# Six places for the down weights, rotations behind the scan pieces, and transposes around the last evaluation in a decoder layer

## The reference

```python
x = x + attn(layernorm(x))                 # 16 heads of 32, 2 key/value heads, rotary, causal softmax, then wo
x = x + mamba(ctx, z=layernorm(x))         # below
x = x + ffn(layernorm(x))                  # below

# mamba: ctx (4, 512, 256) -> inner width 512, 16 states
u  = silu(causal_conv4(ctx @ in_proj.T) + conv_b)
dt, B, C = split(u @ x_proj.T);  dt = softplus(dt @ dt_proj.T + b)
for each position: state = state * exp(dt * A) + (dt * u) * B;  y = sum over 16 states of state * C
y = (y + D * u) * silu(z)

# ffn: hidden 1408 = 11 tiles of 128, 8 experts of rank 16, top 2 per token
g, v = x @ Wg.T, x @ Wu.T
out = (silu(g) * v) @ Wd.T
out += sum over experts e of w_e * 2 * (silu(g + 2*x@Ag_e.T@Bg_e.T) * (v + 2*x@Au_e.T@Bu_e.T)) @ Ad_e.T @ Bd_e.T
```

## Time and profile before

| what | value |
|---|---|
| median of the runs | 1496.59 us |
| the profiled execution, its own time | 1496.58 us |
| its span | 1494.8 us |
| TensorE busy (matmul) | 1345.9 us, 90% |
| VectorE busy | 1028.1 us, 69% |
| ScalarE busy | 695.4 us, 47% |
| down matmuls (L934), 352 records | 164.1 us busy, 17.0 us idle before |
| granted TensorE clock, mean | 0.917 of full |

### The profile page before, as it was taken

One profiled execution on the slowest core, in us unless ns is written; L12 is line 12 of the kernel. 1 busy time (PEld: TensorE's weight loads), 2 busy tenths in 40 slices (PEclk: granted clock), 3 DMA queues, 4 the chain that ended last, 5 costly groups with the idle time before them and its releaser, 6 DMA issues.

```text
span 1494.8 us, 16001 instructions
## 1 busy us (share of the span) xinstructions
PE 1345.9 (90%) x5768; PEld 661.1 (44%) x5768; DVE 1028.1 (69%) x1219; ACT 695.4 (47%) x1477; POOL 89.2 (6%) x116
## 2 busy tenths in 40 slices
PE   5757668999999799899999799899999899799999
PEld 2324444444444365444444365444444355444443
DVE  5699996689979645789897844779897944521110
ACT  5345653465542285375552277365562187121110
POOL 0000001000000000000000000100000000100000
PEclk8955669999999799999999889999999999799999
DMA  6286661157765700137765610117775530012102
GB/s 232 46 197 145 136 146 29 53 138 189 189 148 126 176 2 1 43 106 181 180 162 141 164 45 2 39 53 189 190 166 144 144 83 2 0 33 63 59 25 85
DMA packets 53277, 158.80 MB, mean 106 GB/s; under 512 B 5072, under 2 KB 10704, under 8 KB 44752
## 3 DMA queue, kind: packets, MB, share of 16 engines
q0 software_dynamic: 9216, 67.11, 22.6%
q1 hardware_dynamic: 25664, 54.23, 11.1%
q10 hardware_dynamic: 18320, 36.45, 8.1%
HBM read 86.20 MB, written 4.46 MB: 61 GB/s over the span
## 4 chain that ended last, share of the span: by engine, by line
PE 68%; DVE 20%; ACT 6%; DMA 3%; issue 3%; ACTq 0%; POOL 0%; DVEq 0%
PE ps_a L854 21%; PE ps_a L866 10%; DVE state L1048 7%; PE ps_a L934 6%; PE ps_b L874 5%; PE ps_a L780 4%; PE ps_w L833 4%; PE ps_w L742 4%; PE ps_b L794 3%; DMA y_sb<-state 3%; DVE state L1053 3%; DVE state L1043 3%; ACT r L583 2%; DVE neg_max L1083 2%; PE ps_w L900 2%
## 5 line engine op out<-in xcount | busy, mean ns | idle before, releaser
L854 PE MATMUL ps_a<-xt,w_sb 128*128 128x512 f32 x704 | 319.2, 607 | 0.0
L1048 DVE TENSOR_TENSOR_SCAN state<-decay,state 128x2048 f32<-128x2048 f32 x64 | 282.7, 4418 | 2.1 <-DVE state L1043 0.5
L854 PEld LDWEIGHTS ps_a<-xt,w_sb 128*128 128x128 f32 x704 | 137.2, 196 | 173.2 <-issue 172.8
L635 ACT ACTIVATE r<-ps_a 128x512 f32<-128x512 f32 x132 | 78.8, 597 | 257.5 <-PE ps_a L866 137.5
L583 ACT ACTIVATE r<-ps_a,neg_max 128x128 f32<-128x128 f32 (+3 forms) x256 | 134.6, 542 | 131.8 <-DVE neg_max L1083 126.0
L1219 DVE TENSOR_TENSOR r<-r,ps_a 128x512 f32<-128x512 f32 x132 | 90.2, 685 | 149.9 <-ACT r L635 149.9
L934 PE MATMUL ps_a<-wd_sb,r 128*128 128x512 f32 x352 | 164.1, 617 | 17.0 <-DMA wd_sb<-in_w_down 16.8
L541 ACT ACTIVATE decay<-dt_sb,decay_rate 128x511 f32<-128x511 f32 x256 | 163.4, 711 | 30.1 <-DVE state L1048 29.7
L866 PE MATMUL ps_a<-r,wb_sb 128*128 128x512 f32 x352 | 166.6, 596 | 2.2 <-DVE r L1219 2.2
L780 PE MATMUL ps_a<-r 32*128 32x512 f32 (+3 forms) x512 | 125.7, 572 | 44.1 <-ACT r L583 40.0
L1043 DVE TENSOR_TENSOR state<-du_sb,bc_sb 128x2048 f32<-128x2048 f32 x64 | 146.2, 2284 | 7.8 <-DMA y_sb<-state 5.7
(11 more groups left out here) (117 smaller groups left out, 1385.3 us busy)
## 6 DMA issues: line engine op xcount, KB each, us to landing
y_sb<-state POOLq DMA_DIRECT2D x64, 1024.0 KB, 9.3
bc_sb<-bc_rows ACTq DMA_DIRECT2D x64, 512.0 KB, 6.1
w_sb<-in_w_tiles SPq DMA_DIRECT2D x44, 512.0 KB, 8.7
wd_sb<-in_w_down SPq DMA_DIRECT2D x44, 256.0 KB, 3.2
wb_sb<-in_w_adapt SPq DMA_DIRECT2D x44, 128.0 KB, 2.1
xa<-in_x SPq DMA_DIRECT2D x4, 1024.0 KB, 5.2
out_x<-xb SPq DMA_DIRECT2D x16, 256.0 KB, 8.0
xn_att<-in_ctx_t SPq DMA_DIRECT2D x4, 512.0 KB, 7.9
```

Of the source, the lines that this page charges most:

```text
L854: mm = nc.tensor.matmul(ps_a[:, 2 * (f % 2) + half, :], w_sb[:, slot, at + k * P:at + (k + 1) * P], xt[:, k, :], start=(k == 0), stop=Fals ...
L1048: nc.vector.tensor_tensor_scan(flat, decay[:, n % 2, :, :].rearrange("p j l -> p (j l)"), flat, 0.0, ALU.mult, ALU.add).then_inc(scan_chai ...
```

## The change

There are four edits. (1) The down weights get six places instead of two: the two of `wd_sb` and the four halves of `w_sb`, which is no longer read after the wide matmuls of tiles 9 and 10. Tiles 2 and 3 are loaded when tile 9's wide products are done, tiles 4 and 5 when tile 10's are, the later ones when the matmuls of the tile six before are done. (2) In the first stage and in the middle batches VectorE's `rotate` of a slot stands behind the slot's scan pieces. (3) Of the four transposes of the next input, TensorE does two ahead of the last evaluation's adapter matmuls and two behind them, and ScalarE moves two ahead of the last gate. (4) Where the scan of a state runs in slot `DOWN`, its decay is made in that slot: of all plans this moves one item, the decay of state 10, from the slot of evaluation 31 to slot 33 in `PLAN_NEXT`.

```diff
+WD_RING = 6
@@ plan
-        slots[at["du", 0] if n == 0 else between(at["du", 0] if n == 1 else at["run", n - 2], at["run", n])]["decay"].append(n)
+        first = at["du", 0] if n < 2 else at["run", n - 2]
+        slots[first if n == 0 else DOWN if at["run", n] == DOWN else between(first, at["run", n])]["decay"].append(n)
@@
+        wd_ring = [wd_sb[:, 0, :], wd_sb[:, 1, :], w_sb[:, 1, 0:D], w_sb[:, 1, D:2 * D],
+                   w_sb[:, 0, 0:D], w_sb[:, 0, D:2 * D]]
@@ sync: load_wd
-                if f >= 2:
-                    sp.wait_ge(wd_used, t * FT + f - 1)
+                if f >= WD_RING:
+                    sp.wait_ge(wd_used, t * FT + f - WD_RING + 1)
+                elif f >= 2:
+                    sp.wait_ge(gu_ready, t * EVALS + EVAL_AT[FT - 2 + (f - 2) // 2, 0] + 1)
                 else:
                     sp.wait_ge(scores_ready, t * STEPS + 1)
-                sp.dma_start(wd_sb[:, f % 2, :], w_down[f]).then_inc(wd_loaded[f % 2], 16)
+                sp.dma_start(wd_ring[f % WD_RING], w_down[f]).then_inc(wd_loaded[f % WD_RING], 16)
@@ scalar, middle batches
                 for e in range(EVALS):
+                    if e == EVALS - 1:
+                        transposed("att", "xt", t + 1, False, range(2))
                     if e > 0:
                         evaluate(t, e)
                     load_bc(t + 1, PLAN_NEXT[e])
                     softplus(t + 1, [j for _, j in dt_uses(e)])
                     make_decay(t + 1, PLAN_NEXT[e])
+                transposed("att", "xt", t + 1, False, range(2, NT))
                 for f in range(FT):
-                    if f == 0:
-                        transposed("att", "xt", t + 1, False)
@@ tensor: ffn_tiles
                     if f == FT - 1:
                         down_adapters(t, f - 1)
+                        if b is not None:
+                            transpose_normed("att", "xt", b, False, range(2))
                     add_slot(t, f, 2)
...
                 if b is not None:
-                    transpose_normed("att", "xt", b, False)
+                    transpose_normed("att", "xt", b, False, range(2, NT))
                 down_adapters(t, FT - 1)
                 for f in range(FT):
-                    of_slot = (FT - f % 2 + 1) // 2
-                    pe.wait_ge(wd_loaded[f % 2], 16 * (t * of_slot + f // 2 + 1))
+                    slot = f % WD_RING
+                    of_slot = (FT - slot + WD_RING - 1) // WD_RING
+                    pe.wait_ge(wd_loaded[slot], 16 * (t * of_slot + f // WD_RING + 1))
@@ vector, first stage
             for f in range(FT):
-                rotate(0, f)
                 for piece in PLAN_FIRST[DOWN + f]["dve"]:
                     scan_piece(0, piece)
+                rotate(0, f)
@@ vector, middle batches
                 for f in range(FT):
-                    rotate(t + 1, f)
                     for piece in PLAN_NEXT[DOWN + f]["dve"]:
                         scan_piece(t + 1, piece)
+                    rotate(t + 1, f)
```

More of the change, by code:

```diff
@@ L227, in decoder_layer @@
         wd_sb = sb("wd_sb", [P, 2, D])
+        wd_ring = [wd_sb[:, 0, :], wd_sb[:, 1, :], w_sb[:, 1, 0:D], w_sb[:, 1, D:2 * D],
+                   w_sb[:, 0, 0:D], w_sb[:, 0, D:2 * D]]
+        assert WBASE == 2 * D and FT % 2 == 1
         ctx_sb = xn_att[:, 0:CT, :]
@@ L264, in decoder_layer @@
         wb_loaded = [sem(f"wb_loaded{k}") for k in range(2)]
-        wd_loaded = [sem(f"wd_loaded{k}") for k in range(2)]
+        wd_loaded = [sem(f"wd_loaded{k}") for k in range(WD_RING)]
         stored = sem("stored")
@@ L542, in make_decay, with transposed @@
                                              scale=decay_rate[:, j, n:n + 1]).then_inc(decay_ready, 1)
-            def transposed(kind, name, b, ffn):
-                for i in range(NT):
+            def transposed(kind, name, b, ffn, tiles=range(NT)):
+                for i in tiles:
                     bank = filled(act, (name, i), b, ffn)
@@ L717, in project_dt, with transpose_normed @@
                                      start=True, stop=True).then_inc(work_full[bank], 1)
-            def transpose_normed(kind, name, b, ffn):
+            def transpose_normed(kind, name, b, ffn, tiles=range(NT)):
                 src = xn if ffn else xn_att
-                for i in range(NT):
+                for i in tiles:
                     pe.wait_ge(xn_ready[kind], b * NT + i + 1)
@@ L927, in ffn_tiles @@
                 if b is not None:
-                    transpose_normed("att", "xt", b, False)
+                    transpose_normed("att", "xt", b, False, range(2, NT))
                 down_adapters(t, FT - 1)
                 for f in range(FT):
-                    of_slot = (FT - f % 2 + 1) // 2
-                    pe.wait_ge(wd_loaded[f % 2], 16 * (t * of_slot + f // 2 + 1))
+                    slot = f % WD_RING
+                    of_slot = (FT - slot + WD_RING - 1) // WD_RING
+                    pe.wait_ge(wd_loaded[slot], 16 * (t * of_slot + f // WD_RING + 1))
                     for i in range(NT):
-                        mm = nc.tensor.matmul(ps_a[:, i, :], hb[:, f, i * P:(i + 1) * P], wd_sb[:, f % 2, :],
+                        mm = nc.tensor.matmul(ps_a[:, i, :], hb[:, f, i * P:(i + 1) * P], wd_ring[slot],
                                               start=(f == 0), stop=False, skip_group_check=True)
```

## The result

The changed kernel took 1481.24 us (median of 4 runs, 1477.23 to 1482.85) against 1496.61 us (4 runs, 1494.74 to 1496.68). The ratio is 0.9896, with a 95% interval from 0.9873 to 0.992: 15.4 us faster.

The account below looks back on a forecast made before the run. TensorE and VectorE were taken to end the down stage almost together, VectorE to bound the first attention, TensorE the later ones. Sum: 1496.6 - 6.05 - 21.6 + 10.9 = 1479.8 us, range 1468 to 1488.

Parts of the forecast that it names:

- Rotations behind the pieces: Middle batches' down stage: scan pieces fill VectorE's waits for rotated projections, 7.2 us earlier per batch, 21.6 in three.
- the term put at 0 with bounds of 1 us: TensorE's idle before the last adapters becomes one piece of about 3.6 us: gain 0, bounds -1 to +1 per batch.
- Six places: Down weights: the 5.59 us stall and 2.7 us at low clock go, so TensorE ends at about 495 us.
- the 7.2 us: VectorE's earlier end of each middle down stage, 495.9 against 503.15 us, from moving rotations behind scan pieces.
- First stage: Scan 0 fills the first projection's wait: first maximum at 81.7 instead of 88.16, less 0.4 for the third add, 6.05 us.
- Rival B: Adds become the bound at two places per middle batch and product 4 in the first stage: 1480 to 1492 us, 14%.
- The clock: Three later attention starts: 2.2 us idle before the scores brings 1.2 GHz in all, costing 1.3 + 1.3 + 8.3 = 10.9.
- Transposes and decay 10: Around the last evaluation: ScalarE loses a pair of table loads, the last gate comes earlier, decay 10 is hidden; gain 0.
- A (the clock holds): Full clock at one or more attention starts, each freeing 8.3 us: 1471.5 for one, or 1469; chance 20%.
- C (hidden): Down stage: rotations hold up the projections, VectorE stays as late as before and the reordering gains nothing: 1496 us, 6%.
- D (the low clock lasts): Later attentions stay at 1.2 GHz far longer: 1513 us; slower from 33 us of low clock each; chance 4%.

Follow-up runs that it names:

- e1: The change with VectorE's rotations ahead of the scan pieces again in the three middle batches: 1496.85 us, ratio 1.0019 to the kernel before.
- e4: The change without the moved transposes and without the moved decay 10: 1479.98 us, ratio 0.9909 to the kernel before.
- e10: The change with unread matmuls before the first scores, behind five score steps and ahead of the middle batches' last adapters: 1452.99 us, ratio 0.9694.
- e2: The whole change with two places for the down weights instead of six: 1481.35 us, ratio 0.9906 to the kernel before.
- e5: The change with VectorE's rotations ahead of the scan pieces again in the first stage only: 1481.86 us, ratio 0.9892 to the kernel before.
- e6: The change with the first batch's first wide and adapter weights asked for eight score steps later: 1476.57 us, ratio 0.9857 to the kernel before.
- e9: The change with the first two tiles of wide and adapter weights loaded at the very start: 1475.6 us, ratio 0.9844 to the kernel before.
- e7: The change with three unread matmuls on TensorE before the first scores of the three later attentions: 1475.48 us, ratio 0.9871 to the kernel before.
- e8: The change with unread matmuls before the first scores and behind each of the first five score steps, later attentions: 1456.19 us, ratio 0.9724.
- e12: The kernel before with only the unread matmuls behind score steps 0 to 4 of the three later attentions: 1483.54 us, ratio 0.9892.
- e3: The kernel before with the six places for the down weights and nothing else of the change: 1504.05 us, ratio 1.0076.
- e11: The change with filled attention steps and adapter wait, first weights at the start, unread matmuls before the last batch's feed-forward: 1445.78 us, ratio 0.9639.

## Why the prediction was right, and where it was off

The time was forecast as 1479.8 us and came out as 1481.24. The mechanism was the forecast one, and three terms were each off by 2 to 3.5 us, in part against each other. That the sum came within 1.5 us is partly luck: 3.1 and 3.5 us of missing gain stand against 2.3 us less for the clock and 1.5 that no term had, and the kernel before alone had medians from 1494.27 to 1501.34 us in the three series.

- **Rotations behind the pieces, -21.6: right in mechanism, 18.46 in size.** The time list held nearly piece by piece: one wait at the second rotation (3.31 us, forecast 3.1), no bank wait of TensorE, no scan piece waiting for an add. e1 shows that this edit carries the whole gain. The missing 3.1 us come from the term put at 0 with bounds of 1 us, the idle ahead of the last adapters: I wrote that the four matmuls behind it "can hardly be slower", which is true (2.46 to 3.78 us), and did not ask about the sixteen behind those (8.30, 8.08 and 7.94 us). e4 and e10 both give 67.5 us back.
- **Six places: the stated reason was wrong.** "Without this edit the 7.2 us would mostly stay" fell with e2. I let the last load keep its price of 5.59 us while I moved the transfers that it ran beside. It needed the step that I did take for the adds: who else is on the transfer engines at that moment, in the new order.
- **First stage, -6.05: 2.55.** The first maximum came at 82.51 instead of 81.7, inside the 79.15 to 82.51 of equal programs (e5), so that part of the term was right. The step that failed is the wait for the add of state 2: it cost 3.39 us where I put 0.4. That the first scores release 1.25 MB of loads stood in the code, and I did not set them beside the adds of the new order; an add of 13.2 us lies outside the spread of the earlier trace rows, which has no such loads beside it. Rival B named this very place, product 4 in the first stage, and put 1.1 us on it. e6 and e9 show the cause.
- **The clock, +10.9: 8.6.** Low at the first scores of all three attentions, as expected, with a new stretch in the third that cost 71.17 - 64.25 = 6.9 us (8.3 forecast) and 0.0 and 1.7 us in the other two (1.3 each). I gave the longer idle as the reason. e7 shows that idle to be part of it only: with it filled the clock still fell in two attentions of three. Matmuls behind the first steps hold it in all three, with the idle filled (e8) or, on the kernel before, with its short idle left (e12, 0.63 us in the first attention); on the change with its 2.47 us left this was not run. The rows of the kernel before already spoke against idle alone: its third attention, which keeps the clock, waited 0.92 us ahead of its first scores, the first only 0.60.

```profile
1194.70 0.49 PE L780 MATMUL ps_a<-r 32*128 32x128 f32 x4 [0.92 <-DVE xb L1232]
```

- **Transposes and decay 10, 0:** as forecast in the total, about 1 us per batch against it in the stage. The last gate is multiplied without idle, at 421.65.
- **Rivals.** A (the clock holds) did not come about, but its price of 8.3 us for each attention was near: e8 has 6.3, 7.8 and 6.3 against the change. With the clock held at all three the time is 1456 us, below my range. B (the adds become the bound) gave 1480 to 1492, which has the measured time in it as well; the time alone doesn't refute it, but the rows do for the middle batches, where no scan piece waits for an add. It held in the first stage. C (hidden) was wrong by its own mark: no projection is held up. D (the low clock lasts) was wrong: 20 to 24 us, not 33.

## What to carry to other kernels

When two engines end a stage together, ask which of them has slack inside; the one with waits that other work can fill is the one to reorder, and a stall taken from the other only moves to the edge, where it may cost more than before (e3). Price every transfer on the path by what is issued beside it in the new order, not by its old wait. Before cutting work from a bounding TensorE, look at its granted clock row: where it falls at the start of a sparse stage, a few dense matmuls that nobody reads can be worth more than the edit (25 us here by the medians, 20.4 of them seen in the three stages, for seven added lines).

## What the runs showed of the hardware

**A busy TensorE at 1.2 GHz.** In the change the engine is busy 20.59 of 21.00 us at the start of attention and granted 0.51 on average. Scores on 32 rows are 32 of the 112 records in that window and 11.2 of the busy us; the rest are masks, transposes and values. Once the clock is back the same kinds of matmuls run at 1.00 (the window from 516 to 532 us). So neither a high busy time nor these shapes tell by themselves at which level the engine is. What it did in the first steps does not decide either. These are the first five microseconds of the first and of the third middle attention in the kernel before; at the end of the first window the clock falls, behind the second it stays up:

```profile
504.60:510.00 5.40, 4.00 (x30) 0.98 1.05 235
...
1194.70:1200.00 5.30, 3.90 (x30) 1.00 1.02 225
```

The columns are length, busy time and count of TensorE, granted clock, DMA share, GB/s. In e8 TensorE is busy 5.02 of 5.10 us there (492.9 to 498.0), and the clock holds at all three. The unread matmuls both close the idle between the steps and add dense work, and no run separates the two. The Trainium skill (TensorE: Matmul & The Clock Gate, section "Why this matters for your kernels") asks for no long idle of TensorE between bursts of matmuls. By that rule e7, which fills the idle, should have held the clock; it did in one attention of three in the profiled run, and only with the steps filled as well (e8) in all.

**The kernel before has a spread of its own.** Its 34 runs in the three series went from 1477.85 to 1503.77 us, and its granted clock from 0.928 down to 0.908. e8, e10 and e11, which hold the clock at the attention starts, spread over 3 to 5 us, and e5 and e6, in whose traces it falls at all three, over 0.6 and 2.4. Two of three attentions lose it in the trace of the kernel before. A few runs of a kernel whose clock falls in some runs and not in others say less than their number suggests.

**An accumulating transfer of 1 MB has no one duration:** 7.0 to 10.4 us beside loads of the down weights, 13.2 and 14.0 (e6) beside the first wide weights, at most 10.7 in the same attention without them (e9). The load pays as well: 256 KB took 9.6 and 8.9 us right behind the issue of an add, 3.1 near the end of one (e2). What of it is bandwidth and what is the order in which the packets are served was not measured.
